# A graph layer's edge loop: first two layers on 16 tiles at once, iterations of 64 tiles, one tile of 64 fetched row by row by SyncE

## The reference

```python
h = relu(layernorm(x))
s = h[:, :32] @ W_up_s / sqrt(32);  v = per component h[:, 32:] @ W_up_v / sqrt(32)
t = silu(silu(edge_feats @ A1 + b1) @ A2 + b2) @ A3      # per edge: 8 -> 64 -> 64 -> 128
w0, w1, w2, w3 = split(t)
ss, vs = s[sender], v[sender]                            # the gather
mji = [ss*y_s*w0, (vs . y_v)/sqrt(3)*w3, ss*y_v*w1, vs*y_s*w2]
message = segment_sum(mji, receiver) / 10                # the scatter
out = x + message (scalars) @ W_out_s, message (vectors) @ W_out_v
```

## Time and profile before

| | |
|---|---|
| median of 3 executions | 1958.09 us (1957.93 to 1958.45) |
| the profiled execution | 1958.71 us, span 1956.9 us |
| PE busy, 22470 matmul records | 1772.9 us (91%) |
| weight loads busy | 1341.7 us (69%) |
| VectorE busy | 1341.7 us (69%) |
| POOL busy, 1515 gathers among it | 1446.5 us (74%) |
| ScalarE busy | 441.2 us (23%) |
| mean granted clock of PE | 0.921 |
| moved by DMA | 128.41 MB, mean 66 GB/s |

### The profile page before, as it was taken

The page is one execution under the profiler, slowest core; times in us unless marked ns, Lnnn a source line. Parts: engine busy times, 40 slices in busy tenths (PEclk is TensorE's granted clock), DMA queues, the critical chain, the costliest instruction groups (busy, mean ns, idle before and its releaser), DMA issues.

```text
span 1956.9 us, 61626 instructions
## 1 busy us (share of the span) xinstructions
PE 1772.9 (91%) x22470; PEld 1341.7 (69%) x22470; DVE 1341.7 (69%) x2623; ACT 441.2 (23%) x836; POOL 1446.5 (74%) x1580
## 2 busy tenths in 40 slices
PE   6999899989998999899989989998999899989985
PEld 3677677767776776677677767776776677667763
DVE  5667766766776677676667766676777667766763
ACT  4222222222222222222212222222222222222221
POOL 4777777777777777777777777777777777777774
PEclk8899999999999999899989999999999999999996
DMA  8222222222222222222222222222222222222222
GB/s 238 62 62 58 62 58 62 59 62 58 61 59 63 59 60 61 59 61 60 62 58 61 58 63 59 61 58 62 59 62 60 61 60 59 62 60 61 58 62 97
DMA packets 116919, 128.41 MB, mean 66 GB/s; under 512 B 70818, under 2 KB 89794, under 8 KB 116772
## 3 DMA queue, kind: packets, MB, share of 16 engines
q0 software_dynamic: 48800, 99.49, 18.2%
q1 hardware_dynamic: 67524, 28.62, 5.5%
q10 hardware_dynamic: 576, 0.05, 0.0%
HBM read 121.61 MB, written 6.43 MB: 65 GB/s over the span
## 4 chain that ended last, share of the span: by engine, by line
POOL 54%; issue 19%; PE 18%; DMA 3%; DVE 2%; POOLq 1%; DVEq 1%; ACT 0%; SPq 0%
POOL rows L560 54%; PE pss L826 8%; PE psw L794 3%; PE pss L815 3%; DMA rows<-node_table,src_in 3%; DVE msgs L710 2%; PE ps L780 2%; PE ps L774 1%; PE psx L845 1%; PE psx L837 0%; DVEq L718 0%; POOLq L555 0%; DVE onehot L672 0%; POOLq L557 0%; DVE msgs L708 0%
## 5 line engine op out<-in xcount | busy, mean ns | idle before, releaser
L560 POOL DMA_INDIRECT rows<-node_table,src_in x1515 | 1430.5, 944 | 471.9 <-issue 464.6
L826 PEld LDWEIGHTS pss<-tab_sb,x_sb 128*128 128x128 f32 x4704 | 611.0, 207 | 85.1 <-issue 75.5
L826 PE MATMUL pss<-tab_sb,x_sb 128*128 128x128 f32 x4704 | 640.0, 294 | 0.0
L686 DVE TENSOR_TENSOR x_sb<-picks_in,psx 128x1024 f32<-128x1024 int32 (+1 forms) x294 | 363.5, 1238 | 106.7 <-PE pss L826 106.1
L794 PE MATMUL psw<-a_bd,h 64*128 64x128 f32 x3136 | 301.2, 314 | 123.4 <-DVE msgs L710 121.2
L794 PEld LDWEIGHTS psw<-a_bd,h 64*128 64x128 f32 x3136 | 222.0, 200 | 226.3 <-DVE msgs L710 174.2
L710 DVE TENSOR_TENSOR msgs<-rows,psw 128x768 f32<-128x768 f32 x392 | 371.1, 947 | 0.0
L708 DVE TENSOR_TENSOR msgs<-rows,psw 128x256 f32<-128x256 f32 x392 | 164.9, 421 | 261.7 <-DMA rows<-node_table,src_in 230.0
L595 ACT ACTIVATE h<-ps,b_sb 128x512 f32<-128x512 f32 x196 | 134.7, 687 | 921.5 <-PE ps L780 921.5
L815 PE MATMUL pss<-msgs,onehot 128*32 128x64 f32 (+1 forms) x12544 | 320.9, 247 | 0.0
L815 PEld LDWEIGHTS pss<-msgs,onehot 128*32 128x32 f32 x12544 | 252.8, 116 | 53.1 <-issue 9.4
(11 more groups left out here) (67 smaller groups left out, 381.9 us busy)
## 6 DMA issues: line engine op xcount, KB each, us to landing
rows<-node_table,src_in POOLq DMA_INDIRECT x1515
ef_in<-in_efT SPq DMA_DIRECT2D x98, 64.0 KB
picks_in<-in_picks SPq DMA_DIRECT2D x50, 64.0 KB
xT_sb<-in_xT SPq DMA_DIRECT2D x7, 448.0 KB, 8.2
x_sb<-in_x SPq DMA_DIRECT2D x7, 448.0 KB, 7.4
attr_in<-in_attr SPq DMA_DIRECT2D x98, 32.0 KB
out_T<-xT_sb SPq DMA_DIRECT2D x1, 3136.0 KB, 8.8
node_table<-tab_sb SPq DMA_DIRECT2D x7, 256.0 KB, 3.8
```

What stands on the lines that cost most here:

```text
L560: pool.indirect_dma_start(out=rows[:, QT * p + t, :], out_offset=None, in_=table, in_offset=bass.IndirectOffsetOnAxis(ap=src_in[:, b, at:a ...
L686: dve.tensor_tensor(pick[:, n, :], picks_in[:, :].unsqueeze(1).broadcast_to([P, nt, P]), node_ps[:, n].unsqueeze(2).broadcast_to([P, nt, P ...
L826: last = nc.tensor.matmul(pss[:, o % 2, CH:CH + F], pick[:, t, :], tab_sb[:, t, :], start=False, stop=(p % 2 == 1 and t == PICK_BLOCKS[p + ...
```

## The change

An iteration is now 4 blocks: 64 tiles, 16 quads. There are 25 iterations; the last has 2 blocks, as before (27 tiles with edges). The ring of `rows` keeps its 8 quads (`RING`) and gets one slot more, `SINGLE_SLOT`, and the second half of an iteration uses the ring's slots again. There are four buffers of senders, edge features, attributes and receivers, one for each block.

1. **The tile fetched by SP.** In each iteration but the last, three tiles aren't gathered by POOL: the last of quad 7 and the third of quad 15, which are picks as before (one for each 32 tiles), and the last of quad 15. The latter's 128 sender numbers come to `list_in`; SP loads them into registers 32 at a time and issues 128 DMAs of one row (512 bytes) each, in four groups, with the block loads of the iteration between the groups. It begins when the messages of the iteration before are made. VectorE waits for all four groups before the messages of quad 15.
2. **Two buffers of picks' numbers**, loaded after the first comparison of the picks that follow.
3. **First two layers on 16 tiles at once.** `layer_1` does two matmuls of 512 columns with their 16 rows at partitions 0 and 32 (`a1_bd` holds its weights twice), `layer_2` four of 64 x 64 with 512 columns, one for each quadrant. Both write the two banks of `ps_mlp`, which take the place of `ps1` and `ps2`; each SiLU covers 1024 columns. Both layers and SiLUs stand once in a block instead of twice. `layer_3` takes its operands from the halves where `layer_2` now leaves them. The order on PE within a quad stays.
4. SP waits for its last loads before it ends the loop; the set-up loads four blocks of senders, and the first-layer weights twice.

The core of the diff:

```diff
-BODY = 2
+BODY = 4
 QB = BODY * QUADS
-NJ = -(-N_EDGES // (BLOCK * BODY))
-NB = NJ * BODY
+NB = -(-N_EDGES // (BLOCK * 2)) * 2
+NJ = -(-NB // BODY)
+LAST_QUADS = (NB - (NJ - 1) * BODY) * QUADS
+RING = 2 * QUADS
+HBUF = 2
-PICK_SLOT = QT * QB - 1
+PICK_SLOT = QT * RING - 1
+SINGLE_SLOT = PICK_SLOT + 1
+SINGLE_PART = P // BODY
+PICKS = QB // RING
...
 def quad_gathers(p):
-    return QT - 1 if QT * (p + 1) - 1 == PICK_SLOT else QT
+    if p == QB - 1:
+        return QT - 2
+    return QT - 1 if p % RING == RING - 1 else QT
+def quad_slot(p):
+    return QT * (p % RING) + (1 if p == QB - 1 else 0)
...
-        rows = sb("rows", [P, QT * QB, F])
+        rows = sb("rows", [P, SINGLE_SLOT + 1, F])
-        picks_in = sb("picks_in", [P, P], I32)
+        list_in = sb("list_in", [1, P], I32)
+        picks_in = sb("picks_in", [P, 2, P], I32)
-        ps1 = pb("ps1", [P, 1, 512])
-        ps2 = pb("ps2", [P, 1, 512])
+        ps_mlp = pb("ps_mlp", [P, 2, MLP_HALF])
...
+                    def claim_singles(j):
+                        sp.wait_ge(list_loaded, j * 16 + 16)
+                        sp.sem_inc(singles_claimed, 1)
+                        sp.wait_ge(msgs_ready, j * QB + MSG_CREDIT)
+                        sp.sem_inc(singles_claimed, 1)
+                    def gather_singles(b):
+                        e0 = b * SINGLE_PART
+                        nodes = nc.values_load_multi_w_load_instructions(
+                            list_in[0:1, e0:e0 + SINGLE_PART], engines=[mybir.EngineType.SP], min_val=0, max_val=NPAD - 1,
+                            skip_runtime_bounds_check_because="the senders are node numbers")[1]
+                        for e, node in enumerate(nodes, e0):
+                            sp.dma_start(rows[e:e + 1, SINGLE_SLOT, :], table[bass.ds(node, 1), :]
+                                         ).then_inc(singles_gathered[b], 16)
+                    def load_block(j, b):
+                        last_quad = b * QUADS + QUADS - 1
+                        sp.wait_ge(gathered[last_quad], j * 16 * quad_gathers(last_quad) + 16 * quad_gathers(last_quad))
+                        load_src(j + 1, b)
+                        sp.wait_ge(l1_done, j * BODY + b + 1)
+                        load_ef(j + 1, b)
+                        sp.wait_ge(onehot_ready, j * OCTS + 2 * b + 2)
+                        load_attr(j + 1, b)
+                    def next_picks(j, i):
+                        sp.wait_ge(pick_ready, (j * PICKS + i + 1) * PICK_STEPS + 1)
+                        load_picks(j * PICKS + i + 2, i)
...
                     with sp.Fori(0, NJ - 1) as j:
+                        claim_singles(j)
                         for b in range(BODY):
-                            last_quad = b * QUADS + QUADS - 1
-                            sp.wait_ge(gathered[last_quad], j * 16 * quad_gathers(last_quad) + 16 * quad_gathers(last_quad))
-                            load_src(j + 1, b)
-                            sp.wait_ge(l1_done, j * 2 * BODY + 2 * b + 2)
-                            load_ef(j + 1, b)
-                            sp.wait_ge(onehot_ready, j * 2 * BODY + 2 * b + 2)
-                            load_attr(j + 1, b)
-                        sp.wait_ge(pick_ready, j * PICK_STEPS + 2 * PICK_STEPS)
-                        load_picks(j + 2)
+                            gather_singles(b)
+                            if b == BODY - 1:
+                                load_list(j + 1)
+                            if b > 0:
+                                load_block(j, b - 1)
+                            if b % 2 == 1:
+                                next_picks(j, b // 2)
+                        load_block(j, BODY - 1)
...
-                    def messages(j, p, tiles):
+                    def messages(j, p, tiles, singles):
                         dve.wait_ge(gathered[p], j * 16 * quad_gathers(p) + 16 * tiles)
+                        if singles:
+                            for b in range(BODY):
+                                dve.wait_ge(singles_gathered[b], j * 16 * SINGLE_PART + 16 * SINGLE_PART)
...
-                    def layer_1(j, o):
-                        b, h = divmod(o, 2)
+                    def layer_1(j, b):
                         pe.wait_ge(ef_loaded[b], j * 16 + 16)
-                        pe.wait_ge(h1_ready, j * OCTS + o + HALF_CREDIT)
-                        nc.tensor.matmul(ps1[:, 0, :], a1_bd[:, :], ef_in[:, b, h * MLP_HALF:(h + 1) * MLP_HALF],
-                                         start=True, stop=True).then_inc(l1_done, 1)
+                        pe.wait_ge(h2_ready, j * BODY + b + PAIR_CREDIT)
+                        for h in range(2):
+                            rows_in = slice(32 * h, 32 * h + 2 * EF)
+                            last = nc.tensor.matmul(ps_mlp[:, h, :], a1_bd[rows_in, :], ef_in[rows_in, b, :],
+                                                    start=True, stop=True)
+                        last.then_inc(l1_done, 1)
-                    def layer_2(j, o):
-                        pe.wait_ge(h1_ready, j * OCTS + o + 1 + HALF_CREDIT)
-                        pe.wait_ge(h2_ready, j * OCTS + o + HALF_CREDIT)
-                        nc.tensor.matmul(ps2[:, 0, :], a2_bd[:, :], h1[:, o % 2, :],
-                                         start=True, stop=True).then_inc(l2_done, 1)
+                    def layer_2(j, b):
+                        pe.wait_ge(h1_ready, j * BODY + b + 1)
+                        pe.sem_inc(l2_begun, 1)
+                        for h in range(2):
+                            for g in range(2):
+                                hid = slice(HID * g, HID * (g + 1))
+                                to = slice(HID * (g ^ h), HID * (g ^ h) + HID)
+                                last = nc.tensor.matmul(ps_mlp[to, g, :], a2_bd[hid, hid], h1[hid, h, :],
+                                                        start=True, stop=True)
+                        last.then_inc(l2_done, 1)
```

More of the change, by code:

```diff
@@ L81 @@
 PICKED_CREDIT = 1
-HALF_CREDIT = 2
+PAIR_CREDIT = 1
 def quad_tiles(p):
@@ L218, in gnn_layer_kernel @@
         src_again = sem("src_again")
+        list_loaded = sem("list_loaded")
+        singles_claimed = sem("singles_claimed")
+        singles_gathered = [sem(f"singles_gathered{b}") for b in range(BODY)]
         picks_loaded = sem("picks_loaded")
@@ L613, in iteration @@
                     def iteration(j, first=False, last=False):
-                        for o in range(OCTS):
-                            ahead = (j, o + 2) if o + 2 < OCTS else (j + 1, o + 2 - OCTS)
+                        for o in range(LAST_OCTS if last else OCTS):
+                            b, h = divmod(o, 2)
+                            ahead = (j, b + 1) if b + 1 < BODY else (j + 1, 0)
+                            mlp = h == 0 and not (last and b + 1 >= LAST_BLOCKS)
                             before = not (first and o == 0)
@@ L618, in iteration @@
                                 copy_sums(j, o - 1, not last)
-                            if not (last and o + 2 >= OCTS):
+                            if mlp:
                                 silu_1(*ahead)
@@ L622, in iteration @@
                                 copy_turned(j, o - 1)
-                            if not (last and o + 2 >= OCTS):
+                            if mlp:
                                 silu_2(*ahead)
-                    for o in range(2):
-                        silu_1(0, o)
-                    for o in range(2):
-                        silu_2(0, o)
+                    silu_1(0, 0)
+                    silu_2(0, 0)
                     iteration(0, first=True)
@@ L728, in iteration @@
                     def iteration(j, first=False, last=False):
-                        for p in range(QB):
+                        for p in range(LAST_QUADS if last else QB):
                             g = p // 2 + 1
-                            ahead = (j + g // 4, g % 4) if not (last and 2 * g >= QB) else None
+                            half, r = divmod(p, RING)
+                            ahead = (j + g // OCTS, g % OCTS) if not (last and 2 * g >= LAST_QUADS) else None
                             n = 2 * p - WINDOW_LAG
@@ L865, in iteration @@
                             scatter(j, p)
-                            if half == 0 and not last and p < PICK_STEPS:
+                            if half == 0 and not last and p % RING < PICK_STEPS:
                                 pick_rows(j, p)
-                    for o in range(2):
-                        layer_1(0, o)
-                    for o in range(2):
-                        layer_2(0, o)
+                    layer_1(0, 0)
+                    layer_2(0, 0)
                     layer_3(0, 0)
```

171 lines of the change are left out of this document (95 added, 76 removed).

## The result

The changed kernel takes 1974.89 us (1971.05 to 1977.78, 4 executions), the kernel before, run beside it, 1958.27 us. The ratio is 1.0083, interval 1.0070 to 1.0095: 0.8% **slower**, where 1.5% faster was forecast. The profiled execution takes 1977.78 us, span 1975.9 us, 19.0 us over the span of before.

The account below looks back on a forecast made before the run. POOL's gathers, 1.249 us apart, were taken as the bound: span 1956.9 - 30.0 (gathers) + 0.8 (set-up) = 1927.7 us, forecast 1929 us, other terms hidden. Range 1925 to 2008 us, the forecast's own 1926 to 1934.

Parts of the forecast that it names:

- part 4: Longer loop bodies on PE and VectorE: possible refetch 24 times, even 3 us each covered by PE's idle time; counted as nothing.
- part 3: First two layers in row groups on PE: gain of about 150 us busy time, returning as idle time, moving no end.
- rival A: SyncE becomes the bound through register loads or row transfers, holding back the next claim; slower than before, 27%.
- Part 1: POOL's gathers: one fewer in 64 tiles, 1491 instead of 1515, taking 30.0 us off the path.
- Part 2: 128 row transfers on SyncE at 0.40 us and four register loads at 2 us per iteration, hidden beside POOL.
- the round of 69 us: SyncE's time per iteration, 51 + 8 + 5.0 + 5.2 us, beside POOL's 76.2 us, with 7 us over.
- rival B: SyncE's round falls between 76.2 and 77.6 us, or late transfers delay VectorE near the end: 1935 to 1960 us; 7%.
- Part 5: Set-up: two more sender loads ahead of the first x transfer move everything by about 0.8 us.
- C: Row groups don't overlap, and PE with its fetches takes over in part of each iteration: 1930 to 1955 us; 5%.
- gap in PE or VectorE at each return of the loop: Sign on the timelines of PE or VectorE that would show the longer loops' fetches (part 4) cost time.

Follow-up runs that it names:

- all_4: short_32 with the loops of TensorE, VectorE and ScalarE written out for four iterations (128 tiles): 1932.32 us, ratio 0.9861.
- pe_long: short_32 with TensorE's loop alone written out for two iterations: 1975.76 us, ratio 1.0086.
- unroll_both: Kernel before with only the loops of TensorE, VectorE and ScalarE written out for two iterations of 32 tiles: 1959.65 us, ratio 1.0005.
- long_old: Changed kernel (iterations of 64 tiles, one tile fetched row by row) with the old first two layers: 1965.61 us, ratio 1.0039.
- experiments 7 and 8: short_32 with TensorE's or VectorE's loop alone written out twice: 1975.76 and 1971.44 us; then with TensorE's, VectorE's and ScalarE's loops written out four times: 1932.32 us.
- Experiment 4: Changed kernel with bodies of 32 tiles on TensorE, VectorE and ScalarE, and row transfers in eight groups of 16: 1980.57 us, ratio 1.0114.
- experiments 2 and 5: Kernel before with new layers alone: 1958.68 us; Experiment 4 with four groups of 32 rows, edge features on ScalarE's queue, new or old layers: 1930.93 or 1929.93 us.
- spread: Changed kernel with the second layer and its SiLU one quad later, ahead of the turn that had no layer before it: 1971.22 us, ratio 1.0057.
- experiment 9: Changed kernel with the second layer and its SiLU moved one quad later, so both turns of a block have TensorE work before them: 1971.22 us, ratio 1.0057.
- experiment 6: long_old, 1965.61 us, and the kernel before with new layers and TensorE's, VectorE's and ScalarE's loops written out for two iterations, 1967.84 us, ratio 1.0047.
- short_32: Changed kernel with 32-tile bodies on TensorE, VectorE and ScalarE, four groups of 32 row transfers, edge features on ScalarE's queue: 1930.93 us, ratio 0.9862.

## Why the prediction was wrong

**The step that failed is part 4**, its last sentence: 3 us on PE at a return "would be 72 us of idle time that PE has (the gain of part 3), so the sum has nothing for it". The mechanism and its size were right: q8 went from 11 to 239 packets and TensorE stood 3.6 us at a return. The Trainium skill's "Runtime: NRT & Kernel Launch", section "Instruction fetch mechanics", says that straight code is fetched ahead and that a taken branch out of what is held waits; the trace agrees with both, in all_4 and in pe_long. Wrong was against what I weighed it. TensorE's 143 us of idle time are for the most part waits inside a chain that closes over VectorE in every quad, not time that it has at the return. The largest of them in the kernel before:

```profile
PE psw L794 <- DVE msgs L710: 121.2, 100, 2.6
```

The room is the distance between POOL's 38.7 us and the chain's own time for a round, and no view of the kernel before shows the latter. unroll_both puts it at 36.3 us or less, long_old at 36.9, and the new layers at 37.1 to 37.5: with the old layers 2 x (38.7 - 36.3 or 36.9) = 3.6 to 4.8 us of room in 64 tiles, about what a return takes (3.8 us in the changed kernel, 41.2 - 37.4). So at the old POOL's pace and with the old layers the long bodies cost nothing, as unroll_both shows. At POOL's 38.1 us for a round and with the new layers the room is 2 x (38.1 - 37.4) = 1.4 us, and 3.8 - 1.4 = 2.4 us of each return stand free. The term should have been 22 x (78.6 - 76.2) = 54 us, less some 10 us at the two ends, in place of nothing. Pace and room come from the same rounds, so this sum describes the loss; that the bodies' length causes it rests on experiments 7 and 8.

That the stated range, 1925 to 2008 us, holds 1974.9 us is luck: it was drawn out for rival A, a SyncE that sets the pace, and that isn't what happened.

**Part 1** was right: 1491 gathers, and 28 us less where the chain follows. **Part 2** had both prices right, 0.42 us for 0.40 and 2.06 us for 2, and in the changed kernel VectorE is nowhere seen to wait for the single rows. The load's 64 ns for a register is a third of the 200 ns on that page of the Trainium skill, which speaks of registers that the runtime loads; the 200 ns don't hold for this load, and rival A's high end fell with it. But the round of 69 us was too short. SyncE's loop branches lie 78.4 us apart in the steady part of the changed kernel, 1.9 us of it the wait at the claim, and 76.7 and 77.0 us apart in two early iterations without that wait: its own round is some 76.5 to 77 us, and the margin of 7 us over POOL's 76.2 wasn't there. About 2.7 us of the missing 7.5 are its own fetch at the return (from the branch to the next instruction), 3 us the transfers (54 us for 51); the rest wasn't taken apart. It is what rival B asked of SyncE, and it was hidden only because the chain was slower still. Experiment 4 fell into it with loads twice as many.

**Part 3** had the size right (131 us, range 100 to 190), and that it "moves no end" held in short bodies (experiments 2 and 5). Both of layer 1's matmuls take 1.13 us together where the earlier trace rows have 1.12 for one. That it would "come back as idle time" to cover the fetches did not. **Part 5**: the first gather is at 44.6 us, 2.7 us later and not 0.8; in spread, whose set-up is the same, it is at 43.15 us, 1.3 us later, so half of the excess is the scatter of single executions. **The rivals**: C named TensorE with its fetches, at 5% and 1930 to 1955 us, but tied it to row groups that don't overlap; they do overlap, and it happened all the same. There was no rival "fetches exceed the chain's room", which would have stood on the slower side. The "gap in PE or VectorE at each return of the loop" is the sign that came true.

What stays open is why the new layers lengthen a long-bodied iteration by 0.5 to 1.1 us though TensorE works less. It isn't the turn's wait (experiment 9). The SiLU of 1024 columns takes 1.11 us, and TensorE's clock is at its lower level more often (0.900 for 0.919 in long_old); neither was tried by itself. Open is also why long_old's round without a fetch is longer than unroll_both's (experiment 6).

## What to carry to other kernels

An engine's idle time, and even its wait for the bottleneck, isn't the room for a new stall: ask how long a round of the cyclic chain would take if the bottleneck were faster, and put the stall against that difference. To lengthen a loop body is an edit of its own: look whether the instruction queue has a few packets or some in every iteration, and if it has them, either keep the body short on the engines of the chain or make it so long that many rounds share one return. And try the parts of a change apart: the two that gave nothing here, layers and long bodies, hid the one that gave 1.4%.

## What the runs showed of the hardware

TensorE's loop body of 32 tiles is fetched once: 11 packets. It has some 965 instructions in the trace of the kernel before: 458 matmul records, 458 weight loads (the prediction's 917 are both together) and 49 of its sequencer. A body of 64 tiles, some 1925 in unroll_both and 1956 in the changed kernel, is fetched in each iteration (217 to 239 packets), with 3.3 to 4.4 us of idle TensorE at a return on average. VectorE's stall at the return shown is 2.39 + 1.47 us, spread over two gaps. A load of 32 registers takes 2.06 us.

TensorE's clock falls without any fetch too. In the timeline of short_32, whose body is held, it idles 1.85 us for messages, then works on for 1.5 us, and the same four matmuls take 2.08 us instead of 1.13; the granted clock is 1.00 from 1041 to 1042 us and 0.51 from 1042 to 1045 us:

```profile
1040.85 0.72 PE L877 MATMUL psw<-a_bd,h 64*128 64x128 f32 x8 [1.85 <-DVE msgs L782]
1041.49 0.83 PE L898 MATMUL pss<-msgs,onehot 128*32 128x128 f32 x32
1042.32 2.08 PE L848 MATMUL ps_mlp<-ef_in,a_bd 16*128 16x512 f32 x4
```

With the new layers TensorE is busy 1672.9 us there at a mean granted clock of 0.897, with the old layers in the same form 1759.6 us at 0.937, for the same time within 1.0 us. By an estimate from these numbers, busy time times clock falls by 148 us and busy time by 87: part of the work that the new layers save is given back in clock.
